# VectorE's order at the tail of an attention and mixture-of-experts block: batch 3's shared chunks ahead of batch 1's statistics

## The chip, the cores and the metric

The kernel runs on one core of a Trainium2 chip. The metric is the device time of one execution in microseconds (us). The engines of the core are TensorE (PE; PEld is its weight load), VectorE (DVE), ScalarE (ACT), GpSimd (POOL) and SyncE (SP), which issues most of the DMAs. Each runs its own instruction stream in order and waits on semaphores.

## What is computed

One transformer layer on x of 4 batches x 512 tokens x 256 features, in float32: a linear attention with a residual and a layer norm, then a feed-forward part with a residual and a layer norm. Cut to the feed-forward part, in whose tail the change lies:

```python
router_logits = x @ w_gate                                  # 8 experts
probs = jax.nn.softmax(router_logits, axis=-1)
topk_w, topk_ids = jax.lax.top_k(probs, TOPK)               # 2 of 8
topk_w = topk_w / jnp.sum(topk_w, axis=-1, keepdims=True)
routed = jnp.einsum('te,eth->th', combine, eo)              # weighted sum of two experts per token
shared = _silu_and_mul(x @ w_sh_gate_up) @ w_sh_down        # 256 -> 2 x 512 -> 256
x = _layernorm(x + (routed + shared))
```

## The kernel before, in words

A batch is 4 tiles of 128 tokens (TB = 4), so there are 16 tiles, x1 holds all of them. Matmuls in float32 are made of three products of high and low halves (`split3`, L337 to L341).

**Shared part.** For batch b and chunk c (0 to 3, 128 of the 512 inner features each) TensorE runs `shared_gu(b, c)` (12 matmuls, gate and up), ScalarE `shared_sg` (silu of the gate, L800), VectorE `shared_h` (times up, L1091), ScalarE `shared_hh` (high half, L809), VectorE `shared_lo` (low half, L1098). The product buffer hf has two places, used in turn. When all four low halves of a batch exist (semaphore shl_out), TensorE runs `shared_dn(b, 0)` and `shared_dn(b, 1)`, 48 matmuls, 12 to a tile.

**Routed part.** 39 expert tiles are computed and scattered to y_pairs in DRAM. Then SP loads them back in 8 pair loads of two tiles each into five places (`pair`, L317). `combine(n)` (L1281, 4 instructions on VectorE) adds the two weighted expert outputs of the two tiles of pair n to x1. Pairs 6 and 7, which are batch 3's, are added by TensorE instead (`last_rows`, L514 and L515), in the banks that `shared_dn(3)` then adds to.

**Last layer norm.** For batches 0 to 2 `last_moments(b, ...)` (L1296, L1299) takes mean and variance from x1 on VectorE. For batches 0 and 1 GpSimd then makes scale and shift (`rstd`, L230 to L233, after bn_out) and ScalarE applies them (L932). For batch 2 ScalarE takes the root (`root`, L941), VectorE the reciprocal (`inverse`, L1304) and the shift (L1336, mean_out), and ScalarE applies. For batch 3 VectorE reads the sums from the banks, tile by tile as `shared_dn(3)` gives them, ScalarE takes the root, and VectorE applies (L1307).

**What sets the order.** Everything is written out by hand. ScalarE's stream behind its last `shared_hh(3, 3)` is: a table load for the root, apply batch 0 (4 instructions), apply batch 1 (4), root of batch 2, root of batch 3's first two tiles, apply batch 2 (2), root, apply batch 2 (2), root. SP stores the results (L320) in the order of the batches, two tiles to a DMA for batches 0 to 2 (fin_out), then batch 3's tiles 0 and 1, 2, and 3 (fin_last_out). VectorE's stream is in the function that is printed; the lines that the change touches are L1325 to L1333.

Of the kernel before, what the change touches and what calls it, by code (L numbers as in the profile page):

```python
# [66 lines left out]
def build(nc, xT, x, watt, batt, bq, wffn, wgate, consts, out):  # L67
# [5 lines left out]
    with ctx:  # L73
# [75 lines left out]
        def hh(b):  # L149

            if b % 2 == 0:
                return hh_hi, hh_lo
            return tuple(w[:, :].rearrange("p (c n) -> p c n", c=CS) for w in (wa_hi, wa_lo))
# [804 lines left out]
        def _(dve):  # L958
# [3 lines left out]
            def link(*instructions):  # L962

                for ins in instructions:
                    chain[0] += 1
                    ins.then_inc(S["dve_chain"], 1)
                dve.wait_ge(S["dve_chain"], chain[0])
# [116 lines left out]
            def shared_h(b, c):  # L1084

                i = b * CS + c
                dve.wait_ge(S["sg_out"], i + 1)
                if i >= 2:
                    dve.wait_ge(S["shh_out"], i - 1)
                    dve.wait_ge(S["shl_out"], i - 1)  # L1090
                v.tensor_tensor(hf[:, i % 2, :], bank[2 * (i % 2) + 1][:, :], sg[:, i % 2, :], ALU.mult  # L1091
                                ).then_inc(S["sh_out"], 1)

            def shared_lo(b, c):
                i = b * CS + c
                dve.wait_ge(S["shh_out"], i + 1)
                m_hi, m_lo = hh(b)
                v.tensor_tensor(m_lo[:, c, :], hf[:, i % 2, :], m_hi[:, c, :].bitcast(F32), ALU.subtract  # L1098
                                ).then_inc(S["shl_out"], 1)
# [174 lines left out]
            def combine(n):  # L1274

                dve.wait_ge(pair_in[n], 16)
                dve.wait_ge(S["sres_out"], n + 1)
                for j in reversed(range(TOPK)):
                    for i in range(n * UNIT, (n + 1) * UNIT):
                        r = x1[:, i, 0:D]  # L1280
                        ins = v.scalar_tensor_tensor(r, pair[n][:, i % UNIT, j, :], w_top[:, j, i:i + 1], r,  # L1281
                                                     ALU.mult, ALU.add)
                        if j == 0:
                            ins.then_inc(S["acc_out"], 1)
                    if j:
                        link(ins)

            def last_moments(b, ts):
                for t in ts:
                    r = x1[:, b * TB + t, 0:D]  # L1290
                    if b < NB - 1:
                        dve.wait_ge(S["acc_out"], b * TB + t + 1)
                    else:
                        dve.wait_ge(S["sdn_mm"], 2 * b + t + 1)
                        r = last_sum(t)
                    last = v.bn_stats(stat_end[:, b, t, :], r)  # L1296
                link(last)
                for t in ts:
                    v.bn_aggr(mv[:, b, t, :], stat_end[:, b, t, :]).then_inc(S["bn_out"], 1)  # L1299
# [22 lines left out]
            shared_h(3, 1)  # L1322
            last_moments(0, range(TB))
            shared_lo(3, 1)
            combine(3)  # L1325
            shared_h(3, 2)
            last_moments(1, range(TB))
            shared_lo(3, 2)
            combine(4)
            shared_h(3, 3)  # L1330
            combine(5)
            shared_lo(3, 3)
            last_moments(2, range(TB))  # L1333
            last_moments(3, range(0, 2))
            inverse(2, slice(0, TB), 1)
# [169 lines left out]
```

## Time and profile before

| | us |
|---|---|
| median of 3 runs | 235.03 |
| lowest and highest run | 232.92, 236.46 |
| profiled execution, its time | 232.75 |
| profiled execution, its span | 230.9 |

The profile is of one execution. Its span runs from the first to the last record, and lies within its time, which is 1.85 us longer. Times in the rows are from the start of the span. A row of the timeline gives the start, the duration, engine, line, operation, what it writes and reads, and how many alike stand in a row; where several are merged, the duration is that of the whole group. In brackets stand the idle time of the engine ahead of it and what released it. Consecutive instructions of VectorE and ScalarE overlap by some 0.1 us in the records, so the next start, not the end, tells what a piece costs.

### The profile page before, as it was taken

The numbers are of one execution on the slowest core, as the hardware profiler recorded it, in microseconds if no ns is written. First come the engines' busy times: TensorE is split into PE (matmuls) and PEld (weight loads), VectorE is DVE, ScalarE is ACT, GpSimd is POOL, SyncE is SP. The second block draws the span as 40 slices with busy tenths as digits, with TensorE's granted clock in tenths as the row PEclk, the third lists the DMA queues.
The fourth block names the chain that finished last, engine by engine and source line by source line (L and its number), as shares of the span: only waits on it lengthen the run. The fifth ranks groups of instructions, "written<-read, shape, count | busy, mean of one in ns | idle before, by whom it ended". The sixth has DMA issues, their size and how long they took to land.

```text
span 230.9 us, 4976 instructions
## 1 busy us (share of the span) xinstructions
PE 218.6 (95%) x1428; PEld 191.0 (83%) x1428; DVE 151.6 (66%) x530; ACT 116.6 (50%) x300; POOL 133.6 (58%) x152
## 2 busy tenths in 40 slices
PE   7899999999999999999999989999999999999781
PEld 2468888879888978978799879999999988888681
DVE  2771553525975593865998886666666742689975
ACT  2273441591266083257307177777777763312393
POOL 0047697899877978477678006666666774003300
PEclk9999999999999999999999999999999999999999
DMA  5973484333131122022255246666666520973036
GB/s 154 375 236 88 109 303 125 94 92 91 44 95 47 49 92 93 0 93 93 92 183 185 58 107 173 186 165 178 178 178 180 147 95 4 374 232 123 0 134 232
DMA packets 21404, 31.59 MB, mean 137 GB/s; under 512 B 3200, under 2 KB 14081, under 8 KB 21380
## 3 DMA queue, kind: packets, MB, share of 16 engines
q1 hardware_dynamic: 17424, 22.33, 32.6%
q0 software_dynamic: 3408, 8.43, 10.4%
q10 hardware_dynamic: 548, 0.53, 0.8%
q8 instruction: 13, 0.21, 0.4%
q14 instruction: 11, 0.09, 0.2%
HBM read 19.56 MB, written 12.62 MB: 139 GB/s over the span
## 4 chain that ended last, share of the span: by engine, by line
PE 79%; DVE 11%; ACT 4%; DMA 3%; issue 2%; SPq 0%; DVEq 0%; ACTq 0%
PE bank L339 18%; PE bank L341 17%; PE bank L340 16%; PE bank L639 4%; PE bank L381 3%; PE bank L540 3%; DMA xt_raw<-in_xT 3%; PE bank L666 2%; PE bank L459 2%; PE bank L669 2%; PE bank L667 2%; PE bank L395 2%; DVE x L1281 2%; PE bank L657 2%; PE bank L448 2%
## 5 line engine op out<-in xcount | busy, mean ns | idle before, releaser
L1441 POOL DMA_INDIRECT y_pairs<-x_t,dst x39 | 38.0, 973 | 28.0 <-DVE dst L1174 24.1
L1404 POOL DMA_INDIRECT x_slots<-x,slot x32 | 32.3, 1010 | 10.2 <-issue 9.0
L339 PE MATMUL bank<-x1t_hi,wf_hi 128*128 128x512 f32 x64 | 26.2, 410 | 0.7 <-DVE xt_raw L1091 0.5
L339 PE MATMUL bank<-wf_hi,ot_hi 128*128 x78 | 25.3, 324 | 0.4 <-DVE ot_lo L1176 0.4
L341 PE MATMUL bank<-x1t_hi,wf_lo 128*128 128x512 f32 x64 | 25.3, 395 | 0.0
L340 PE MATMUL bank<-x1t_lo,wf_hi 128*128 128x512 f32 x64 | 25.2, 394 | 0.0
L1385 POOL TENSOR_TENSOR wf_lo<-stage,wf_hi 128x512 fp32r<-128x512 f32 x18 | 23.2, 1289 | 1.4
L756 ACT ACTIVATE k_sb<-bank,cst 128x256 f32<-128x256 f32 x16 | 7.7, 481 | 29.6 <-PE bank L356 27.1
L341 PE MATMUL bank<-wf_hi,ot_lo 128*128 x78 | 22.0, 282 | 0.0
L340 PE MATMUL bank<-wf_lo,ot_hi 128*128 x78 | 21.9, 280 | 0.0
L1174 DVE SCALAR_TENSOR_TENSOR dst<-o_sb,te_f 128x1 f32 (+1 forms) x39 | 8.5, 219 | 16.0 <-ACT ot_hi L870 15.9
L800 ACT ACTIVATE xt_raw<-bank 128x512 f32<-128x512 f32 x16 | 9.5, 596 | 14.6 <-PE bank L341 14.6
L870 ACT CAST ot_hi<-bank 128x256 fp32r<-128x256 f32 x39 | 14.7, 377 | 4.2 <-PE bank L639 4.0
L885 ACT COPY x_t<-bank 128x256 f32<-128x256 f32 x39 | 14.5, 373 | 3.5 <-PE bank L669 1.5
L1176 DVE TENSOR_TENSOR ot_lo<-bank,ot_hi 128x256 fp32r<-128x256 f32 x39 | 16.3, 417 | 0.0
L875 ACT ACTIVATE q_t<-bank 128x128 f32<-128x128 f32 x39 | 10.9, 278 | 10.3 <-PE bank L341 9.6
L1091 DVE TENSOR_TENSOR xt_raw<-bank,xt_raw 128x512 f32<-128x512 f32 x16 | 11.0, 685 | 7.0 <-ACT xt_raw L800 6.8
L339 PEld LDWEIGHTS bank<-wf_hi,ot_hi 128*128 128x128 f32 x78 | 14.7, 188 | 1.0 <-issue 0.6
L639 PE MATMUL bank<-cst,o_sb 128*128 128x128 f32 x78 | 15.0, 274 | 0.3 <-DMA o_sb<-x_slots 0.3
L339 PEld LDWEIGHTS bank<-x1t_hi,wf_hi 128*128 128x128 f32 x64 | 12.1, 189 | 3.3 <-issue 0.6
L340 PEld LDWEIGHTS bank<-wf_lo,ot_hi 128*128 128x128 f32 x78 | 14.8, 190 | 0.0
L230 POOL TENSOR_SCALAR nw<-mv 128x4 f32<-128x4 f32 x6 | 2.1, 351 | 21.9 <-DVE mv L1299 19.1
(185 smaller groups left out, 685.0 us busy)
## 6 DMA issues: line engine op xcount, KB each, us to landing
o_sb<-x_slots SPq DMA_DIRECT2D x39, 129.0 KB
stage<-in_wffn SPq DMA_DIRECT2D x18, 256.0 KB, 2.7
x<-in_x SPq DMA_DIRECT2D x4, 512.0 KB, 6.8
out<-x SPq DMA_DIRECT2D x7, 256.0 KB, 2.5
xt_raw<-in_xT SPq DMA_DIRECT2D x3, 512.0 KB, 6.7
x_slots<-fill SPq DMA_DIRECT2D x9, 129.0 KB, 2.9
x<-in_watt SPq DMA_DIRECT2D x4, 256.0 KB, 6.0
k_sb<-y_pairs SPq DMA_DIRECT2D x2, 512.0 KB, 3.9
```

The source lines that it names most:

```text
L339: mm(o, w_hi, m_hi, start=start, stop=False, **more)
L340: mm(o, w_hi, m_lo, start=False, stop=False, **more)
L341: return mm(o, w_lo, m_hi, start=False, stop=stop, **more)
L639: last = nc.tensor.transpose(o[:, k * P:(k + 1) * P], xg[:, u, k * P:(k + 1) * P], ident)
L870: copy(xe_hi[:, u, :, :], xe_bank(u).rearrange("p (k n) -> p k n", k=KD)).then_inc(S["xe_hi_out"], 1)
L875: activation(eg[:, u % 2, :], bank[u % 2][:, 0:IM], ACT.Silu).then_inc(S["eg_out"], 1)
L885: copy(ey[:, u, :], y_bank[:, 0:D]).then_inc(S["ey_out"], 1)
L1091: v.tensor_tensor(hf[:, i % 2, :], bank[2 * (i % 2) + 1][:, :], sg[:, i % 2, :], ALU.mult).then_inc(S["sh_out"], 1)
L1176: v.tensor_tensor(xe_lo[:, u, :, :], xe_bank(u).rearrange("p (k n) -> p k n", k=KD), xe_hi[:, u, :, :].bitcast(F32), ALU.subtract).then_in ...
L1385: g.tensor_tensor(wf_lo[:, c], stage[:, i % 2, :], wf_hi[:, c].bitcast(F32), ALU.subtract).then_inc(S["wf_split"], 1)
L1404: pool.indirect_dma_start(out=x_scat, out_offset=bass.IndirectOffsetOnAxis(ap=slot[:, j, t:t + 1], axis=0), in_=x1[:, t, :], in_offset=Non ...
L1441: pool.indirect_dma_start(out=y_scat, out_offset=bass.IndirectOffsetOnAxis(ap=dst[:, j:j + 1], axis=0), in_=ey[:, u, :], in_offset=None, b ...
```

## The change

The tail of VectorE's program is put in another order. No instruction is added or removed, and no other engine's program changes.

```diff
             shared_h(3, 1)
             last_moments(0, range(TB))
             shared_lo(3, 1)
+            shared_h(3, 2)
             combine(3)
-            shared_h(3, 2)
+            shared_lo(3, 2)
+            shared_h(3, 3)
+            combine(4)
+            shared_lo(3, 3)
             last_moments(1, range(TB))
-            shared_lo(3, 2)
-            combine(4)
-            shared_h(3, 3)
             combine(5)
-            shared_lo(3, 3)
             last_moments(2, range(TB))
             last_moments(3, range(0, 2))
             inverse(2, slice(0, TB), 1)
```

On VectorE, from the low half of chunk (3, 1) on (L1098 is a low half, L1091 a product with bank1 for chunk (3, 2) and bank3 for (3, 3), L1281 from q_t is `combine(3)`), there stood before:

```order
L1098 TENSOR_TENSOR wa_lo<-xt_raw,wa_hi 128x512
L1281 SCALAR_TENSOR_TENSOR x1<-q_t,w_top,x1 128x256 x4
L1091 TENSOR_TENSOR xt_raw<-bank1,xt_raw 128x512
L1296 BN_STATS stat_end<-x1 128x6 x4
L1299 BN_AGGR mv<-stat_end 128x2 x4
L1098 TENSOR_TENSOR wa_lo<-xt_raw,wa_hi 128x512
```

and now there stands:

```order
L1098 TENSOR_TENSOR wa_lo<-xt_raw,wa_hi 128x512
L1091 TENSOR_TENSOR xt_raw<-bank1,xt_raw 128x512
L1281 SCALAR_TENSOR_TENSOR x1<-q_t,w_top,x1 128x256 x4
L1098 TENSOR_TENSOR wa_lo<-xt_raw,wa_hi 128x512
L1091 TENSOR_TENSOR xt_raw<-bank3,xt_raw 128x512
```

The product of chunk (3, 2) stands ahead of `combine(3)`, and its low half directly behind that, no longer behind the statistics of batch 1.

Directly behind those rows, still on VectorE and up to the statistics of batch 2 (L1281 from o_sb is `combine(4)`, from k_sb `combine(5)`; a pair of L1296 and L1299 is the statistics of one batch), there stood before:

```order
L1281 SCALAR_TENSOR_TENSOR x1<-o_sb,w_top,x1 128x256 x4
L1091 TENSOR_TENSOR xt_raw<-bank3,xt_raw 128x512
L1281 SCALAR_TENSOR_TENSOR x1<-k_sb,w_top,x1 128x256 x4
L1098 TENSOR_TENSOR wa_lo<-xt_raw,wa_hi 128x512
L1296 BN_STATS stat_end<-x1 128x6 x4
L1299 BN_AGGR mv<-stat_end 128x2 x4
```

and now:

```order
L1281 SCALAR_TENSOR_TENSOR x1<-o_sb,w_top,x1 128x256 x4
L1098 TENSOR_TENSOR wa_lo<-xt_raw,wa_hi 128x512
L1296 BN_STATS stat_end<-x1 128x6 x4
L1299 BN_AGGR mv<-stat_end 128x2 x4
L1281 SCALAR_TENSOR_TENSOR x1<-k_sb,w_top,x1 128x256 x4
L1296 BN_STATS stat_end<-x1 128x6 x4
L1299 BN_AGGR mv<-stat_end 128x2 x4
```

The last low half, of chunk (3, 3), now stands ahead of `combine(5)` and of batch 1's statistics, and these stand behind it. Batch 2's statistics stay behind all of it.

## Rows read from the trace of the kernel before

**Rows 1.** Page, part 1: busy time, share of the span, instructions.
```profile
PE 218.6 (95%) x1428; PEld 191.0 (83%) x1428; DVE 151.6 (66%) x530; ACT 116.6 (50%) x300; POOL 133.6 (58%) x152
```

**Rows 2.** Waits from 205 us on: engine, line, releaser, total, times, longest.
```profile
PE bank L339 <- DVE wa_lo L1098: 2.3, 1, 2.3
```

**Rows 3.** Timeline of TensorE: last matmul of `shared_gu(3, 3)`, last of `last_rows`, first of `shared_dn(3, 0)`.
```profile
212.33 0.39 PE L341 MATMUL bank<-x1t_hi,wf_lo 128*128 128x512 f32 x1
...
217.31 0.59 PE L515 MATMUL bank<-x,cst 128*128 128x256 f32 x2
220.18 0.36 PE L339 MATMUL bank<-wf_hi,wa_hi 128*128 128x256 f32 x1 [2.28 <-DVE wa_lo L1098]
```

**Rows 4.** Timeline of VectorE from `combine(3)` to the statistics of batch 2.
```profile
210.73 1.79 DVE L1281 SCALAR_TENSOR_TENSOR x<-q_t,w_top,x 128x256 f32<-128x256 f32 x4
212.44 0.68 DVE L1091 TENSOR_TENSOR xt_raw<-bank,xt_raw 128x512 f32<-128x512 f32 x1
213.04 1.40 DVE L1296 BATCH_NORM_STATS2 stat_end<-x 128x6 f32<-128x256 f32 x4
214.47 0.38 DVE L1299 BATCH_NORM_AGGREGATE mv<-stat_end 128x2 f32<-128x6 f32 x4
214.77 0.66 DVE L1098 TENSOR_TENSOR wa_lo<-xt_raw,wa_hi 128x512 fp32r<-128x512 f32 x1
...
217.65 1.79 DVE L1281 SCALAR_TENSOR_TENSOR x<-k_sb,w_top,x 128x256 f32<-128x256 f32 x4
219.36 0.68 DVE L1098 TENSOR_TENSOR wa_lo<-xt_raw,wa_hi 128x512 fp32r<-128x512 f32 x1
219.96 1.40 DVE L1296 BATCH_NORM_STATS2 stat_end<-x 128x6 f32<-128x256 f32 x4
```

**Rows 5.** Timeline of ScalarE in the tail.
```profile
209.98 0.60 ACT L800 ACTIVATE xt_raw<-bank 128x512 f32<-128x512 f32 x1 [0.82 <-PE bank L341]
213.16 0.62 ACT L809 CAST wa_hi<-xt_raw 128x512 fp32r<-128x512 f32 x1 [2.58 <-DVE xt_raw L1091]
...
218.40 1.28 ACT L943 ACT_TABLE_LOAD   x1
...
219.81 4.03 ACT L932 ACTIVATE x<-x,nw 128x256 f32<-128x256 f32 x8
223.74 0.64 ACT L941 ACTIVATE nw<-mv,eps_ln 128x4 f32<-128x4 f32 x2
224.47 1.09 ACT L932 ACTIVATE x<-x,nw 128x256 f32<-128x256 f32 x2
```

**Rows 6.** Timeline of GpSimd: `rstd` of an earlier batch (first row), and of batch 1 in the tail.
```profile
95.75 0.24 POOL L230 TENSOR_SCALAR nw<-mv 128x4 f32<-128x4 f32 x1 [2.55 <-DVE mv L1061]
...
214.94 0.58 POOL L230 TENSOR_SCALAR nw<-mv 128x4 f32<-128x4 f32 x1 [2.15 <-DVE mv L1299]
...
217.19 0.20 POOL L233 TENSOR_TENSOR nw<-nw 128x4 f32<-128x4 f32 x1
```

**Rows 7.** Timeline of VectorE behind the statistics of batch 2.
```profile
221.90 0.43 DVE L1296 BATCH_NORM_STATS2 stat_end<-bank 128x6 f32<-128x256 f32 x1
223.33 0.43 DVE L1296 BATCH_NORM_STATS2 stat_end<-bank 128x6 f32<-128x256 f32 x1 [1.01 <-PE bank L341]
...
224.06 0.18 DVE L1304 RECIPROCAL nw<-nw 128x4 f32<-128x4 f32 x1
224.27 0.16 DVE L1336 SCALAR_TENSOR_TENSOR nw<-mv,nw 128x4 f32<-128x4 f32 x1
224.78 0.43 DVE L1296 BATCH_NORM_STATS2 stat_end<-bank 128x6 f32<-128x256 f32 x1 [0.34 <-PE bank L341]
```

**Rows 8.** Timeline of SP: the store of batch 2's last tiles, then two of batch 3's three.
```profile
226.76 0.37 SPq L320 DMA_DIRECT2D out<-x  x1
...
227.18 0.47 SPq L320 DMA_DIRECT2D out<-x  x1
...
228.36 0.34 SPq L320 DMA_DIRECT2D out<-x  x1
```

**Rows 9.** Stretch of the end: length, busy PE, PEld, DVE, ACT, POOL, PEclk, DMA share, GB/s.
```profile
228.00:229.00 1.00, 0.00 (x0) 0.00 (x0) 0.33 (x1) 0.00 (x0) 0.00 (x0) 1.00 1.02 344
```

## The prediction

> **What bounds the kernel now.** I read the page's busy times first: TensorE is busy for 95% of the span [rows 1]. So a change on VectorE alone can only bring what TensorE waits for, and what lies behind its last matmul. The waits from 205 us on name one of TensorE: 2.3 us for VectorE's low half [rows 2]. The timeline puts it between the last matmul of `last_rows`, which ends at 217.31 + 0.59 = 217.90, and `shared_dn(3, 0)` at 220.18 [rows 3]: 2.28 us for shl_out. On VectorE there is no idle time in brackets from `combine(3)` at 210.73 to batch 2's statistics at 219.96, and the last low half ends at 219.36 + 0.68 = 220.04 [rows 4]. TensorE starts 0.14 us behind it. So in this stretch VectorE's order is the bound.
>
> **What the change moves, step by step.** Each slot is the distance to the next start. A product costs 213.04 - 212.44 = 0.60 us, a combine 212.44 - 210.73 = 1.71, the statistics of a batch 214.77 - 213.04 = 1.73, a low half 219.96 - 219.36 = 0.60 [rows 4]. The new order from 210.73 on:
>
> - h(3, 2) at 210.73. Its silu runs on ScalarE from 209.98 for 0.60 us [rows 5], so it is there at 210.58, with 0.15 us to spare.
> - combine(3) at 211.33, next start 213.04. Its pair was loaded long before, as its old start was the same engine's next free moment.
> - lo(3, 2) at 213.04. ScalarE's cast follows the start of its product by 213.16 - 212.44 = 0.72 and takes 0.62 [rows 4, 5], so it ends at 210.73 + 0.72 + 0.62 = 212.07, in time.
> - h(3, 3) at 213.64. TensorE ends `shared_gu(3, 3)` at 212.33 + 0.39 = 212.72 [rows 3]; with the silu of 0.60 that is about 213.36, with 0.28 us to spare.
> - combine(4) at 214.24; lo(3, 3) at 215.95. Its cast is over at 213.64 + 1.34 = 214.98.
>
> The last low half so starts at 215.95 and not at 219.36, 3.4 us earlier, which is the 1.71 of combine(5) and the 1.73 of the statistics that it no longer stands behind. It is ready for TensorE at 215.95 + 0.68 + 0.14 = 216.77. TensorE is in `last_rows` until 217.90, so **its wait of 2.28 us goes whole**, and `shared_dn(3)` starts and ends 2.28 us sooner. The 1.1 us between 216.77 and 217.90 is the reserve: this step holds if any one of the hand-overs above is late by less.
>
> **What is late next.** VectorE has the same work, only permuted. Batch 1's statistics run from 216.55, combine(5) from 218.28, batch 2's statistics from 219.99 as before, and the first bank of batch 3 is read at 221.9 as before [rows 7], although TensorE now has it at about 219.6. So VectorE gives nothing back up to here. Behind that it saves the wait of 1.01 us for the second bank: I place the second read 0.35 us behind the first (four such take 1.40 [rows 4]), at 222.25, and the reciprocal 224.06 - 223.33 = 0.73 later [rows 7], at 222.98. VectorE alone could then be 1.08 us sooner at the reciprocal.
>
> But that reciprocal also waits for ScalarE's root, and here the moved statistics have a price. Batch 1's statistics started at 213.04 and now start at 216.55. GpSimd's chain started 214.94 - 213.04 = 1.90 us behind that, and took 217.19 + 0.20 - 214.94 = 2.45 us [rows 4, 6]. It is now over at 216.55 + 1.90 + 2.45 = 220.90. ScalarE's table load follows the last cast and starts 3.4 us sooner, near 214.99; batch 0 is applied from 1.41 us behind it (219.81 - 218.40), from 216.4 to about 218.4. There ScalarE stands and waits for batch 1's scale, which before was long made. Applying costs (223.74 - 219.81) / 8 = 0.49 us a tile [rows 5], so batch 1's four tiles and with them the root of batch 2 come at 220.90 + 0.04 + 4 x 0.49 = 222.90, where before it was 223.74: **0.84 us sooner, not 2.28**. The reciprocal, 0.32 us behind the root's start (224.06 - 223.74 [rows 5, 7]), is at 223.22, later than the 222.98 that VectorE could do. So this chain (statistics of batch 1, GpSimd, ScalarE's four tiles, root) is the one that sets the end now.
>
> Then shift, apply batch 2 and its stores follow as before, all 0.84 sooner: the store of batch 2's last tiles is issued at 226.76 - 0.84 = 225.92. VectorE's own tail, with the third bank long there, is read once the shift is made, at 224.27 + 0.16 - 0.84 = 223.59, where it was 224.78, 1.2 us sooner. It gains 0.35 us more than the stores. But SP issues in order, at 0.4 to 0.5 us a store (226.76, 227.18 and 0.47 long [rows 8]). Three more after 225.92 come to 227.3 to 227.4 for the last, against 228.36. That is 1.0 sooner. And the DMA engines are full from 228 on (share 1.02, 344 GB/s [rows 9]), in a burst that the store of batch 2 opens, so I count its 0.84 and not the 1.0.
>
> **The sum.** Bounds of the gain: 2.28 us if all of TensorE's wait came through, 1.0 by the last store's issue, 0.84 by the burst. I take 0.85. The profiled execution would go from 232.75 to 231.9 and its span from 230.9 to 230.05. That execution is 2.3 us under the median, and the three runs lie 3.5 us apart, so the change is smaller than their scatter. On the median: 235.03 x 231.9 / 232.75 = 234.2 us.
>
> [...] GpSimd's first instruction of the chain took 0.58 us in the tail, beside a low half of VectorE, and 0.24 earlier in the kernel [rows 6]. It started at 214.94 inside the low half of 214.77 to 215.43 and ended at 215.52, just behind it [rows 4, 6]. The rest of the chain ran beside combine(4) and still came to 2.45 us in all. The combine beside it took 1.71, like the one at 217.65 with no GpSimd work beside it [rows 4]. [...] In the new order the chain lies beside combine(5), four instructions of two SBUF inputs each. If each of its four instructions had to wait out a whole one of 0.43 us (1.71 / 4), the chain would take 2.11 + 4 x 0.43 = 3.8 us, where 2.11 is 2.45 less the 0.34 of the first. By the rows it is 2.1 to 2.45. I take 2.45, since combine(4) is the nearest neighbour that the trace has.
>
> **The rivals.**
> - *The whole wait comes through*: 2.3 us, 232.7 us on the median. For it speaks that the chain that ended last runs through TensorE's matmuls behind the wait. Against it, that VectorE is at work without a gap until 221.9, and that the reciprocal cannot come 1.1 us sooner even if ScalarE were free. Chance 0.07.
> - *Nothing comes of it*: 235.0. VectorE's sum of work is the same, and a hand-over that is some tenths late (the silu of chunk (3, 2) has 0.15 to spare, that of (3, 3) 0.28) shifts all behind it, the statistics of batch 1 and 2 too, one for one. If both are missed by 0.4, the gain of 0.85 is gone. Chance 0.2.
> - *Slower*: GpSimd's chain is stretched beside combine(5), to 3.8 us as above, 1.35 more than in the sum. The root comes at 222.90 + 1.35 = 224.25, 0.5 later than before, and so does every store: 235.5 us. It decides from a chain of 2.45 + 0.85 = 3.3 us on. Chance 0.08.
> - *The forecast*, a gain of 0.4 to 1.3 us: 0.65.
>
> **How the numbers follow.** All four cases lie between 232.7 and 235.5 on the median. The scatter of the runs is added: the lowest and the highest of the runs, each less 0.85, are 232.1 and 235.6. I give 232.0 to 235.8. Two per cent are 4.7 us, about what a measurement of this kernel can tell from no change. No case reaches that, since the wait that can be removed is 2.28 us; 0.03 and 0.02 are left for a shift between the two measurements. So the verdict should be no difference.
>
> **What would show it.** In the new profile: TensorE's wait for the low half is gone, and `shared_dn(3, 0)` starts at 217.9 in place of 220.18. ScalarE shows a wait of about 2.5 us for GpSimd ahead of batch 1's first tile, at 220.9. The root of batch 2 starts at 222.9, the store of batch 2's last tiles at 225.9 and the last at 227.4; VectorE's two waits for TensorE's banks are gone. The sum is wrong if the span falls by 2 us (then the chain over GpSimd does not bind), if GpSimd's chain takes more than 3 us, or if VectorE shows a wait for a silu of over 0.3 us.

## The result and the profile after

| | before | changed |
|---|---|---|
| median of 19 runs each, us | 234.57 | 232.40 |
| lowest and highest run | 232.25, 238.86 | 231.30, 235.60 |
| profiled execution, its time and span | 232.75, 230.9 | 233.38, 231.6 |
| tail: start of the product of (3, 1) to the end of the span | 230.9 - 207.82 = 23.1 | 231.6 - 209.45 = 22.1 |

The tail so runs from the start of VectorE's product of chunk (3, 1) to the end of the span. The granted clock of TensorE, where it is given below, is a share of full speed as the profile gives it: 1.00 is full and 0.50 is half; over a stretch or a span it is the mean.

The ratio of the changed kernel to the one before is 0.9926, with a 95% interval of 0.9897 to 0.9955: 0.74% faster, 1.7 us of 234.57. A ratio compares only the runs that lie within 1.5% of the fastest run of their kernel, so it is not that of the medians, which lie 2.17 us apart. The gain is within 2%, so the verdict is no difference, as forecast. It is more than the 0.85 us of the forecast, and 0.85 us (0.9964) lies just outside the interval.

The profiled execution of the changed kernel has the longer span of the two, and yet the shorter tail. Its tail starts 209.45 - 207.82 = 1.63 us later than that of the first. Matched instruction by instruction, TensorE lost most of that between 131 and 165 us (0.25 us behind at 131, 2.06 at 165), in the expert tiles, whose code is the same. So times of the two tails are compared here with 1.63 us taken off the new ones.

Timeline of TensorE in the changed kernel, where [rows 3] had the wait:

```profile
218.94 0.59 PE L515 MATMUL bank<-x,cst 128*128 128x256 f32 x2
219.18 0.47 PE L339 MATMUL bank<-wf_hi,wa_hi 128*128 128x256 f32 x1
219.49 0.28 PE L340 MATMUL bank<-wf_lo,wa_hi 128*128 128x256 f32 x1
```

The first matmul of `shared_dn(3, 0)` has no idle time ahead of it. It is at 219.18 - 1.63 = 217.55, 2.6 us sooner. The second is at 219.49 - 1.63 = 217.86 and was at 220.38, and from there to the last all are 2.5 us sooner.

Timeline of VectorE in the same stretch, as [rows 4] and [rows 7]:

```profile
212.36 0.68 DVE L1091 TENSOR_TENSOR xt_raw<-bank,xt_raw 128x512 f32<-128x512 f32 x1
...
217.58 0.68 DVE L1098 TENSOR_TENSOR wa_lo<-xt_raw,wa_hi 128x512 fp32r<-128x512 f32 x1
218.18 1.40 DVE L1296 BATCH_NORM_STATS2 stat_end<-x 128x6 f32<-128x256 f32 x4
219.62 0.38 DVE L1299 BATCH_NORM_AGGREGATE mv<-stat_end 128x2 f32<-128x6 f32 x4
219.91 1.77 DVE L1281 SCALAR_TENSOR_TENSOR x<-k_sb,w_top,x 128x256 f32<-128x256 f32 x4
221.59 1.40 DVE L1296 BATCH_NORM_STATS2 stat_end<-x 128x6 f32<-128x256 f32 x4
...
223.32 0.73 DVE L1296 BATCH_NORM_STATS2 stat_end<-bank 128x6 f32<-128x256 f32 x2
...
224.79 0.18 DVE L1304 RECIPROCAL nw<-nw 128x4 f32<-128x4 f32 x1 [0.45 <-ACT nw L941]
```

The last low half is at 217.58 - 1.63 = 215.95, to the hundredth where the sum put it, and batch 2's statistics are at 219.96 as before. The two reads of batch 3's banks run back to back now. What VectorE waits for instead is ScalarE's root, 0.45 us.

Timeline of ScalarE, and of GpSimd ahead of it:

```profile
220.08 0.38 POOL L230 TENSOR_SCALAR nw<-mv 128x4 f32<-128x4 f32 x1 [5.67 <-DVE mv L1299]
...
222.26 0.20 POOL L233 TENSOR_TENSOR nw<-nw 128x4 f32<-128x4 f32 x1
```

```profile
218.03 2.06 ACT L932 ACTIVATE x<-x,nw 128x256 f32<-128x256 f32 x4
222.49 2.08 ACT L932 ACTIVATE x<-x,nw 128x256 f32<-128x256 f32 x4 [2.40 <-POOL nw L233]
224.48 0.47 ACT L941 ACTIVATE nw<-mv,eps_ln 128x4 f32<-128x4 f32 x2
```

The wait for GpSimd is the new one: 2.40 us. The root of batch 2 is at 224.48 - 1.63 = 222.85, 0.89 us sooner than the 223.74 of [rows 5]. SP's store of batch 2's last tiles follows:

```profile
227.49 0.37 SPq L320 DMA_DIRECT2D out<-x  x1
```

That is at 225.86, 0.90 us sooner than in [rows 8], and the span ends 0.9 us sooner. The tail did what the sum said. What the sum does not hold is the other 0.8 us of the 1.7.

### The profile page after: what moved, and what is told of

Its sections match the earlier page's. It is cut to its first block, busy times and chain, and to the rows that moved or that the text cites. A ratio compares the mean times of both kernels' runs of the same rounds, so it can differ in the third digit from the quotient of the medians.

```text
span 231.6 us, 4976 instructions
## 1 busy us (share of the span) xinstructions
PE 218.9 (95%) x1428; PEld 191.0 (82%) x1428; DVE 152.6 (66%) x530; ACT 116.6 (50%) x300; POOL 133.6 (58%) x152
## 4 chain that ended last, share of the span: by engine, by line
PE 72%; DVE 11%; DMA 6%; ACT 5%; issue 3%; POOL 1%; SPq 1%; POOLq 0%; DVEq 0%; ACTq 0%
PE bank L339 16%; PE bank L341 15%; PE bank L340 15%; DMA o_sb<-x_slots 4%; PE bank L381 3%; PE bank L540 3%; PE bank L639 3%; DMA xt_raw<-in_xT 2%; PE bank L459 2%; PE bank L395 2%; PE bank L666 2%; PE bank L448 2%; PE bank L669 2%; PE bank L667 2%; PE bank L657 2%
## 5 line engine op out<-in xcount | busy, mean ns | idle before, releaser
L1091 DVE TENSOR_TENSOR xt_raw<-bank,xt_raw 128x512 f32<-128x512 f32 x16 | 11.0, 685 | 6.9 <-ACT xt_raw L800 6.8
L340 PEld LDWEIGHTS bank<-wf_lo,ot_hi 128*128 128x128 f32 x78 | 14.8, 190 | 0.0
## 6 DMA issues: line engine op xcount, KB each, us to landing
stage<-in_wffn SPq DMA_DIRECT2D x18, 256.0 KB, 2.9
out<-x SPq DMA_DIRECT2D x7, 256.0 KB, 2.1
x<-in_watt SPq DMA_DIRECT2D x4, 256.0 KB, 6.2
```

Of the source, the lines that this page charges most:

```text
L340: mm(o, w_hi, m_lo, start=False, stop=False, **more)
```

## The experiments

Three theories. **Theory 1**: the chain from batch 1's statistics over GpSimd and ScalarE to the root of batch 2 sets the end of the tail, the tail is 0.9 us shorter, and the rest of the difference is scatter. **Theory 2**: time is saved ahead of the tail too. **Theory 3**, formed after the first four runs: TensorE's wait also lets its clock fall in part of the executions.

### The two kernels again

No edit in either.

> The changed kernel once more. The tail from the product of chunk (3, 1) to the end of the span was 230.9 - 207.82 = 23.1 us before and 231.6 - 209.45 = 22.1 in the changed profile, 0.9 less; the 19 runs each had fast runs 0.74% apart, which is 1.7 us. Theory 1 (only the tail changed, the rest is scatter of the expert stage): tail of 22.1 again, ratio 0.996, that is 0.9 us. Theory 2 (the change saves time elsewhere too): ratio 0.9925 and a stretch ahead of the tail that is shorter by some 0.8 us in trace after trace.

Measured: ratio 0.9937 (0.9892 to 0.9982), tail 232.3 - 210.23 = 22.1 us. Its span is longer than the first one's, for the expert tiles came later again. Matched by instruction with the first profile of before, the two profiles of the changed kernel are 0.27 and 0.00 us behind it at 100 us, and 1.63 and 2.42 us from 191 us on. No stretch ahead of the tail is shorter by 0.8 us in both, so Theory 2 has nothing for it. The 0.7%, however, came back (0.63%).

> The kernel before once more, against itself. Tail of 23.1 us in the trace and ratio 1.000 by both theories; how far the ratio lies from 1 tells how much of 0.7% can be scatter.

Measured: ratio 1.0024 (0.9978 to 1.0071), so scatter between two sets is 0.2% here. But the tail was not 23.1. It was 235.1 - 210.62 = 24.5 us. Timeline of TensorE in this profile, from the end of the wait on:

```profile
222.98 0.36 PE L339 MATMUL bank<-wf_hi,wa_hi 128*128 128x256 f32 x1 [2.28 <-DVE wa_lo L1098]
223.17 0.28 PE L340 MATMUL bank<-wf_lo,wa_hi 128*128 128x256 f32 x1
...
223.92 0.42 PE L340 MATMUL bank<-wf_lo,wa_hi 128*128 128x256 f32 x1
224.13 0.42 PE L341 MATMUL bank<-wf_hi,wa_lo 128*128 128x256 f32 x1
...
227.30 0.28 PE L341 MATMUL bank<-wf_hi,wa_lo 128*128 128x256 f32 x1
```

and its stretches (length, busy PE, PEld, DVE, ACT, POOL, granted clock, DMA share, GB/s):

```profile
219.00:222.00 3.00, 1.70 (x8) 1.14 (x6) 2.93 (x8) 1.43 (x2) 1.10 (x2) 1.00 0.00 0
222.00:225.00 3.00, 2.02 (x13) 2.05 (x14) 2.52 (x10) 2.99 (x7) 0.00 (x0) 0.81 0.12 43
225.00:228.00 3.00, 3.00 (x18) 3.00 (x18) 0.81 (x2) 1.81 (x5) 0.00 (x0) 0.63 0.77 268
228.00:231.00 3.00, 2.46 (x21) 2.25 (x19) 2.39 (x11) 2.61 (x6) 0.00 (x0) 1.00 0.24 83
```

A stretch of 1 us from within the third:

```profile
225.10:226.10 1.00, 1.00 (x7) 1.00 (x7) 0.43 (x1) 1.00 (x4) 0.00 (x0) 0.50 0.76 268
```

In the first profile of before the clock stayed up behind the same wait:

```profile
222.00:225.00 3.00, 3.00 (x27) 3.00 (x27) 1.57 (x7) 2.85 (x8) 0.00 (x0) 1.00 0.71 240
```

The wait is the same 2.28 us. Some 0.8 us behind it the matmuls start 0.21 us apart and no longer 0.12, and some 3.4 us later they are back. The granted clock was 0.50 in between (the stretch from 225.10) and 1.00 on either side. VectorE then waits 0.67 and 1.96 us for the banks, where the first profile of before had no more than 1.01 [rows 7]:

```profile
225.23 0.43 DVE L1296 BATCH_NORM_STATS2 stat_end<-bank 128x6 f32<-128x256 f32 x1 [0.67 <-PE bank L341]
227.62 0.43 DVE L1296 BATCH_NORM_STATS2 stat_end<-bank 128x6 f32<-128x256 f32 x1 [1.96 <-PE bank L341]
```

The price is 24.5 - 23.1 = 1.4 us. In the 29 runs of before that these sets share, the mean granted clock is 0.991 or less in 17 and 0.995 or more in 12, with none between; in the 12 runs of this set it is 0.992 or less in 9 and 0.996 or more in 3. The profile whose clock stayed up has a mean of 0.998, the one whose clock fell 0.991.

The mean is to be read with care, and only within one kernel. In all fourteen profiles of this case the clock also falls to 0.50 in the last microseconds of the span, 2.1 to 4.5 us behind the end of TensorE's last matmul, where TensorE has no work left, and the mean over the span holds that too. The kernel before has only some 4.7 us there; other orders have more (some 8 us in the run with the doubled chain below, whose mean is 0.989 although its clock was up to the last matmul).

### One part alone, and the other

```diff
             combine(3)
             shared_h(3, 2)
-            last_moments(1, range(TB))
             shared_lo(3, 2)
             combine(4)
             shared_h(3, 3)
             combine(5)
             shared_lo(3, 3)
+            last_moments(1, range(TB))
             last_moments(2, range(TB))
```

> One part alone: batch 1's statistics moved behind the last low half, products and low halves where they were, combine(5) still ahead of the last low half. Theory 1 (the chain of batch 1's statistics, GpSimd, ScalarE's four tiles and the root of batch 2 sets the end): TensorE's wait falls from 2.3 to 0.6 us, the statistics start 1.7 us later than in the changed kernel, the root of batch 2 0.8 us later than before, the tail is 23.9 us, ratio 1.003. Rival (what TensorE no longer waits comes through at the end): tail 21.4, ratio 0.993.

Measured: ratio 1.0018 (0.9968 to 1.0067), tail 233.0 - 208.81 = 24.2 us, the root of batch 2 17.1 us behind the product of (3, 1). Timeline of VectorE, and of ScalarE:

```profile
214.80 0.69 DVE L1098 TENSOR_TENSOR wa_lo<-xt_raw,wa_hi 128x512 fp32r<-128x512 f32 x1 [0.68 <-ACT wa_hi L809]
```

```profile
223.89 2.08 ACT L932 ACTIVATE x<-x,nw 128x256 f32<-128x256 f32 x4 [1.96 <-POOL nw L233]
225.88 0.47 ACT L941 ACTIVATE nw<-mv,eps_ln 128x4 f32<-128x4 f32 x2
```

TensorE's wait fell from 2.28 to 1.35 us, and the tail grew by 1.1 us over the undisturbed one of before. This rules out the rival, by which TensorE's start decides (it has 21.4 us). I had expected 23.9 us and a wait of 0.6: a low half directly behind its product waits 0.68 us for ScalarE's cast, which I had left out. That the ratio is only 1.002 with a tail 1.1 us longer would fit the clock: in this one profile it did not fall while TensorE had matmuls left.

```diff
             shared_lo(3, 1)
+            shared_h(3, 2)
             combine(3)
-            shared_h(3, 2)
             last_moments(1, range(TB))
             shared_lo(3, 2)
+            shared_h(3, 3)
             combine(4)
-            shared_h(3, 3)
+            shared_lo(3, 3)
             combine(5)
-            shared_lo(3, 3)
             last_moments(2, range(TB))
```

> The other part alone: products and low halves sooner, with batch 1's statistics left where they were in time (behind combine(3)), so that the last low half comes 1.7 us sooner than before and not 3.4. TensorE waits 0.6 us. Theory 1: GpSimd's chain is over at 217.4 on the clock of before and ScalarE has no wait for it; the root of batch 2 comes straight behind its statistics, VectorE's reciprocal 1.08 us sooner than before; tail 22.0 us, as short as the changed kernel's or 0.2 shorter, although TensorE starts its last 48 matmuls 0.6 us later. Rival (TensorE's start decides): tail 0.6 us longer than the changed kernel's, 22.7.

Measured: ratio 0.986 (0.9786 to 0.9933, from six runs, two of them far off: 236.2 us, and 274 us with a mean clock of 0.749, whose cause was not looked into), tail 229.8 - 208.31 = 21.5 us. TensorE waits 0.57 us and still the tail is 0.6 us shorter than the changed kernel's. Timeline of VectorE:

```profile
221.88 0.38 DVE L1299 BATCH_NORM_AGGREGATE mv<-stat_end 128x2 f32<-128x6 f32 x4
222.17 0.73 DVE L1296 BATCH_NORM_STATS2 stat_end<-bank 128x6 f32<-128x256 f32 x2
222.94 0.25 DVE L1299 BATCH_NORM_AGGREGATE mv<-stat_end 128x2 f32<-128x6 f32 x2
223.10 0.14 DVE L1304 RECIPROCAL nw<-nw 128x4 f32<-128x4 f32 x1
```

There is no wait here at all: VectorE is the bound. Its reciprocal is 14.8 us behind the product of (3, 1), 1.45 us sooner than before (16.24), where I had 1.08. The read of the first bank comes 0.29 us behind the start of the aggregates, in [rows 7] it came 0.51 behind: 0.22 us of that was a wait for TensorE which the row does not mark (the last of the bank's twelve matmuls ended at 221.85, the read began at 221.90). Another 0.15 us is a shorter way from the reads to the reciprocal.

### GpSimd's chain, doubled

```diff
             for b in range(EARLY_B):
                 pool.wait_ge(S["bn_out"], (b + 1) * TB)
+                if b == EARLY_B - 1:
+                    link(rstd(g, link, slice(b, b + 1)))
                 rstd(g, link, slice(b, b + 1)).then_inc(S["ln_out"], 1)
```

> The changed kernel, with GpSimd's four instructions for batch 1's scale and shift run twice (same values), about 2.1 us more in that chain. Theory 1: ScalarE's wait for GpSimd grows from 2.4 to 4.5 us, the root of batch 2 comes 17.1 us behind the product of (3, 1) in place of 15.0, and the tail grows by the same 2.1 us to 24.2. Rival (VectorE or TensorE is the bound of the tail): tail 22.1 to 22.4.

Measured: tail 232.0 - 207.86 = 24.1 us. Timeline of ScalarE:

```profile
222.93 2.08 ACT L932 ACTIVATE x<-x,nw 128x256 f32<-128x256 f32 x4 [4.43 <-POOL nw L233]
224.91 0.47 ACT L941 ACTIVATE nw<-mv,eps_ln 128x4 f32<-128x4 f32 x2
```

The wait grew by 2.03 us, the root by 2.02 (17.05 against 15.03 us behind the product), the tail by 2.0. Theory 1 holds for the tail: in the changed kernel the end of the span moved by as much as this chain was made longer. This is one profile with no ratio.

### TensorE's wait, filled and restored

```diff
+            for _ in range(10):
+                mm(bank[5][:, :], heat[:, 0:P], heat[:, :], start=True, stop=True)
             shared_dn(3, 0)
             shared_dn(3, 1)
```

> The kernel before, with ten matmuls of zeros (as the ones at its start) into bank 5, which nothing reads any more, ahead of TensorE's wait for the last low half, so that TensorE works on through the 2.28 us in which it stood. In a second profile of the kernel before, TensorE's clock fell to half 0.8 us behind the end of that wait and stayed there for 3.4 us; shared_dn(3) took 1.4 us longer and the tail was 24.5 us, not 23.1. In 17 of 29 timed runs of before the mean granted clock was 0.991 or less, in the other 12 it was 0.995 or more, with none between. Theory 3 (a wait of 2.28 us lets the clock fall in about half of the executions, and this is the part of the measured gain that the tail of 0.9 us does not explain): the clock stays at full level in shared_dn(3), tail 23.1 to 23.4 us in the profile, and ratio about 0.996, though no wait and no work was taken away. Theory 1 (the rest was scatter of the expert stage): ratio 1.000.

Measured: ratio 0.9935 (0.9892 to 0.9977), tail 235.2 - 212.19 = 23.0 us. Timeline of TensorE and the stretches:

```profile
222.11 2.32 PE L722 MATMUL bank<-heat 128*128 128x512 bf16 x10
224.55 0.36 PE L339 MATMUL bank<-wf_hi,wa_hi 128*128 128x256 f32 x1
```

```profile
222.00:225.00 3.00, 2.88 (x16) 1.36 (x14) 2.96 (x9) 2.84 (x5) 0.00 (x0) 1.00 0.00 0
225.00:228.00 3.00, 3.00 (x28) 3.00 (x27) 1.83 (x9) 3.00 (x7) 0.00 (x0) 1.00 0.50 171
```

`shared_dn(3)` waits for the same low half and starts no sooner (12.36 us behind the product of (3, 1) in both kernels), yet the kernel is 0.65% faster, and the interval leaves out the 1.000 of Theory 1. Its mean clock was 0.994 or more in 12 of 13 runs, against 9 of 17 of the kernel before beside it. Its profiled execution had a span of 235.2 us all the same: its tail began 212.19 - 207.82 = 4.4 us later than in the first profile of before, and 3.3 us of that arose between 131 and 180 us, in the expert tiles. So that stage scatters by more than the gain, at full clock.

> The kernel before, a further profile. Theory 3: either a tail of 23.1 us with the clock at full level in the last 48 matmuls, or one of 24.5 us with the clock at half for some 3.4 us of them; nothing between. Theory 1: tail 23.1.

Measured: tail 234.5 - 209.97 = 24.5 us, the clock down in the same place (0.70 and 0.73 in the stretches from 222 and from 225 us; the wait ended at 222.33), and a mean clock of 0.991. This is one execution, of 236.27 us.

```diff
+            pe.wait_ge(S["acc_out"], 3 * TB)
             shared_dn(3, 0)
             shared_dn(3, 1)
```

> The changed kernel with one wait put back: TensorE waits for combine(5) (all of acc_out) ahead of shared_dn(3), so that it stands idle for about 2.3 us in the place where the kernel before stood, while nothing else of the change is undone. Theory 3 (such a wait lets the clock fall in about half of the executions): either the clock stays full, with VectorE waiting for the banks as before and a tail near 23.1 us, or it falls to half in shared_dn(3), and the tail is near 24.5; over 12 runs the ratio is 1.000 to 1.003, and about half of the runs have a mean granted clock of 0.991 or less. Theory 1 without the clock: tail 23.1 in every profile, ratio 1.000 only if the 1.7 us of the changed kernel were no more than 0.9, so 0.996 to 0.998 against 0.9926 plus 0.9 us.

Measured: tail 261.6 - 237.16 = 24.4 us, ratio 1.0004 (0.9933 to 1.0076). Timeline of TensorE, and a stretch as above:

```profile
249.44 0.41 PE L339 MATMUL bank<-wf_hi,wa_hi 128*128 128x256 f32 x1 [2.19 <-DVE x L1282]
249.66 0.40 PE L340 MATMUL bank<-wf_lo,wa_hi 128*128 128x256 f32 x1
```

```profile
249.00:252.00 3.00, 2.56 (x13) 2.56 (x14) 2.08 (x9) 1.81 (x4) 1.08 (x2) 0.61 0.17 59
```

With an idle time of 2.19 us put back by another wait, the clock is down again, this time from 0.2 us behind the start of the first matmul on (0.50 from 249.7 to 253.1). The ratio is the one expected, but its interval is too wide to tell 1.000 from 0.9965. These runs were on a chip on which every kernel, the one before too, took 27 us more (median of before 262.2 us). The 26 us by which its changed profile (below) is longer than the first changed one arose ahead of the tail, 16 of them between 123 and 191 us, in the expert tiles, and 8 between 110 and 123. The mean clock is lower there in all kernels and does not sort the runs, so the expected share of executions in which the clock falls was not tested. In all four profiles taken on that chip TensorE also stood idle for 5.6 us between 114 and 121 us; the granted clock fell to 0.50 within that idle time and stayed there for 3.0 to 5.7 us behind its end. What made that chip slower was not looked into. Its tails can be compared, its ratios hardly.

### The changed kernel a third time, and a better order

> The changed kernel beside the three others on one chip. Tail 22.1 us, ratio 0.9925 to 0.994 by theory 3 (0.9 us in every execution, 1.4 more in about half of them), 0.996 by theory 1.

Measured on that chip: ratio 0.9965 (0.991 to 1.002), tail 257.7 - 235.60 = 22.1 us. The tail is the one expected. The ratio lies at the 0.996 of Theory 1, and its interval holds the values of both theories.

```diff
             shared_h(3, 3)
+            last_moments(1, range(TB))
+            shared_lo(3, 3)
             combine(4)
-            shared_lo(3, 3)
-            last_moments(1, range(TB))
             combine(5)
```

(against the changed kernel)

> Another order, meant to join what the two parts brought: products and low halves sooner, batch 1's statistics directly behind the product of chunk (3, 3), then the last low half, then combine(4) and combine(5). The last low half starts 216.0 on the clock of before, so TensorE has no wait, and GpSimd's chain is over at 218.6, so ScalarE has nearly none. Theory 1 with VectorE as the next bound: root of batch 2 14.2 us and reciprocal 14.8 us behind the start of the product of (3, 1), as in the run with the products alone; tail 21.5 us, ratio 0.987. If TensorE's earlier start mattered too, the tail would be up to 0.6 shorter than in that run.

Measured: ratio 0.989 (0.9824 to 0.9957, six runs, of which five lay within 231.16 to 231.43 us), tail 229.3 - 207.79 = 21.5 us, reciprocal 14.80 us behind the product of (3, 1). Timeline of ScalarE and of TensorE:

```profile
218.79 2.08 ACT L932 ACTIVATE x<-x,nw 128x256 f32<-128x256 f32 x4 [0.36 <-POOL nw L233]
221.78 0.30 ACT L941 ACTIVATE nw<-mv,eps_ln 128x4 f32<-128x4 f32 x1 [0.91 <-DVE mv L1299]
```

```profile
217.53 0.47 PE L339 MATMUL bank<-wf_hi,wa_hi 128*128 128x256 f32 x1
```

Now ScalarE waits for VectorE's statistics, no longer the other way round, and TensorE waits for nothing. TensorE's start is 0.9 us sooner than with the products alone (9.74 against 10.65 us behind the product of (3, 1)), and the reciprocal and the end are where they were there. TensorE's start is worth nothing beyond that point.

> Batch 1's statistics directly behind the product of chunk (3, 3), again, since the first time gave six runs. Tail 21.5 us as in the first profile; ratio 0.990, the same as the run with the products alone, since VectorE's reciprocal comes 14.8 us behind the product of (3, 1) in both.

Measured on the slower chip: tail 256.0 - 234.49 = 21.5 us, ratio 0.9986 (0.9939 to 1.0033).

> Products and low halves sooner, statistics of batch 1 left behind combine(3), again, since the first time gave six runs. TensorE's wait of 0.6 us is short; theory 3: it lets no clock fall, and the ratio is that of the changed kernel less 0.6 us, 0.990. Rival: the clock falls in part of the runs here too, ratio 0.993 or above and runs with a clock of 0.991 or less with 1.4 us more.

Measured on the slower chip: tail 255.5 - 233.99 = 21.5 us, ratio 0.9965 (0.9915 to 1.0015). The tails are the same to 0.1 us as on the other chips. The ratios do not separate the two orders from the changed kernel, nor, there, from the kernel before, and both miss the 0.990 that I expected: it lies below both intervals. The means over all runs, divided by that of before (35 runs), are 1.002 with the wait restored, 0.994 for the changed kernel, and 0.992 (products alone) and 0.991 for the two orders. That is the order of the tails, and no more than a hint.

## Why the prediction was right, and where it was short

- **TensorE's wait goes whole**: right, and worth a little more than the 2.28 us of the prediction, 2.5 us for all matmuls from the second on. The last low half was at 215.95 as worked out, and the hand-overs that could have been late were not.
- **VectorE gives nothing back up to 221.9; the moved statistics send the end through GpSimd**: right. GpSimd's chain took 222.46 - 220.08 = 2.38 us (2.45 in the sum), ScalarE's wait was 2.40 (about 2.5), the root 0.89 us sooner (0.84), the store 0.90 (0.84), the tail 0.93 (0.85). Doubling the chain moved the end by 2.0 us, so it was the bound and not beside it.
- **Slower through GpSimd beside combine(5)**: did not come. The third instruction of the chain took 1.25 us in place of 1.12, the first 0.38 in place of 0.58. The first instruction ended 0.10 us behind the end of the combine instruction beside which it began (219.91 + 0.45 = 220.36), as it ended 0.09 us behind the low half in the kernel before. In the run with the statistics alone, with no combine beside it, that instruction took 0.23 us. That it is held until VectorE's instruction ends is my reading of these two ends, and no run tests it. The 3.8 us of this rival has each of the chain's four instructions wait out a whole combine instruction of 0.43 us; no run shows that. Of the other three none paid it: in the run with the statistics alone, where the chain had no combine beside it, it took 1.94 us, only 0.44 less.
- **VectorE alone could be 1.08 us sooner at the reciprocal**: too small, 1.45 by the run with the products alone. It bound nothing in the changed kernel, so this error had no price.
- **The sum of 0.85 us for the kernel**: short by half. The step that failed is the price of TensorE's wait. I took from [rows 3] that its only price is 2.28 us of which 0.84 comes through, and worked it out on an execution whose clock happened to stay up. In both further profiles of the kernel before, and in the one of the changed kernel with such a wait restored, the clock fell behind it, and the tail was 24.4 to 24.5 us and not 23.1. In none of the ten profiles without an idle time of 2 us in that place (0, 0.57, 0.58 and 1.35 us, and the filled one) did it fall in the tail before TensorE's last matmul.
- **How much of the other 0.8 us is the clock**: an estimate. If the clock falls in the executions of before whose mean clock is 0.992 or less (17 of 29, 9 of 12 and 8 of 17 on the two faster chips, 34 of 58), that is 0.59 x 1.4 = 0.8 us on the average, and 0.93 + 0.8 = 1.7 us is what was measured. The times of these runs bear it out in part. The runs with the low mean clock are longer by 0.74, 2.05 and 0.60 us in the mean of the three sets, 0.9 us together (0.2 to 1.6, worked out by resampling the runs), where 1.4 was to be expected; but in the 29 the medians of both groups are 234.7 and 234.8. The profiles and the filled wait (0.9935, 1.5 us) are what shows the effect; its size per execution is known (1.4 us), its share is not.
- **The range held with some luck**: the median of 232.40 us lies 1.8 us under the forecast of 234.2, which started from 235.03, a median of three runs, where 19 runs gave 234.57. It lies 0.4 us inside the lower end of the range.

The traces show the granted clock at 0.50 behind a wait of 2.28 us in two of three profiles of the one kernel, and behind one of 2.19 us in the one profile of the other; so a wait of this length was enough, and not each time. Only behind the 2.19 us were the matmuls of the next piece 0.21 us apart from its start; behind the 2.28 us they started 0.12 us apart and were 0.21 apart from 0.8 us on.

## What to carry to other kernels

A wait of TensorE like these, of over 2 us, is to be priced twice: once by what waits behind it (0.9 us of tail here), and once by its clock (1.4 us of tail here, in two of the three profiles of the kernel before). One profile in which the clock stayed up does not show the second price; look at the mean clock of all runs, and at a second profile, before a sum is made. When a piece is moved behind another to free an engine, follow it to its own readers: here the statistics that made room for the last low half fed a chain of 2.4 us over GpSimd and 2 us on ScalarE, and an order that kept them ahead of the last low half had TensorE free and a tail 0.6 us shorter still.

## What the runs showed of the hardware

- TensorE's granted clock fell from 1.00 to 0.50 behind an idle time of 2.28 us: 0.8 us after it ended in two profiles, 0.2 us after in another with 2.19 us idle, and not before the last matmul in a third with 2.28. With 0.57 and 0.58 us (one profile each) and 1.35 us (one) it did not fall while TensorE had matmuls left. It stayed down for some 3.4 us while the matmuls ran without a gap, 0.21 us apart and not 0.12. With ten matmuls of zeros in the wait it stayed up in the one profile, and the mean was 0.994 or more in 12 of 13 runs.
- A wait of VectorE of 0.22 us stood in no bracket of the trace; it was seen only when it was gone. It showed as an idle time of 0.13 us between two records (221.77 to 221.90) where such records else overlap by 0.09.
- The kernel before took 27 us longer on one chip than on the two others. In the changed kernel 16 of 26 us of that were in the expert tiles, and its tail took the same 22.1 us.
- Four small instructions of GpSimd (128x4) took 1.94 us with no combine beside them on VectorE, and 2.38 beside `combine(5)`.
